# Attention of a decoder block: probabilities and values exchanged through DRAM, with the scores of two steps as four products in a row

## The reference

```python
scale = DIM_HEAD ** (-0.5)                      # DIM_HEAD = 64, HEADS = 16
xn = layer_norm(x, ln_g, ln_b)                  # [32, 112, 256]
cn = layer_norm(context, cln_g, cln_b)          # [32, 375, 256]
q = (xn @ Wq).reshape(b, n, HEADS, DIM_HEAD).transpose(0, 2, 1, 3) * scale
k, v = jnp.split(cn @ Wkv, 2, axis=-1)          # one head of keys and values for all 16
sim = jnp.einsum('bhid,bjd->bhij', q, k) + mask[:, None, :, :]
attn = jax.nn.softmax(sim, axis=-1)
out = jnp.einsum('bhij,bjd->bhid', attn, v)
out = out.transpose(0, 2, 1, 3).reshape(b, n, INNER) @ Wout
h = xn @ W1
val, gate = jnp.split(h, 2, axis=-1)
out = out + jax.nn.silu(gate) * val @ W2
```

## Time and profile before

| | |
|---|---|
| median of 3 runs | 2093.75 us (2090.76 to 2095.71) |
| the profiled execution's own time | 2093.83 us |
| its span from first to last instruction | 2092.0 us |
| TensorE busy | 1724.8 us, 82% |
| VectorE busy | 1346.2 us, 64% |
| ScalarE busy | 974.7 us, 47% |
| mean share of the 16 DMA engines on the kernel's queue | 37.1% |

### The profile page before, as it was taken

How to read it: one execution, slowest core, us unless ns; L and a number is a source line. 1 busy time by engine, 2 the same in 40 slices (tenths; PEclk the granted TensorE clock), 3 DMA queues, 4 the chain that set the end, 5 groups by cost and what they waited for, 6 DMA issues and landing times. The chain is left out here.

```text
span 2092.0 us, 25897 instructions
## 1 busy us (share of the span) xinstructions
PE 1724.8 (82%) x7880; PEld 908.4 (43%) x7880; DVE 1346.2 (64%) x3972; ACT 974.7 (47%) x2262; POOL 419.4 (20%) x569
## 2 busy tenths in 40 slices
PE   5579999999996668878878877887888787888786
PEld 2447676676663223333333333333433333333355
DVE  6888999899656555655466465556646656564643
ACT  3355445544335455445455544545544554453541
POOL 4867686768500100000000000000000000000000
PEclk8789999999997879989899989999999999899998
DMA  3000000000144654545454554544554455454531
GB/s 126 1 18 10 27 10 27 19 28 2 35 147 117 185 125 118 130 103 127 121 130 108 142 117 116 133 118 120 124 127 112 117 125 128 107 124 116 118 82 37
DMA packets 153005, 197.33 MB, mean 94 GB/s; under 512 B 56513, under 2 KB 113793, under 8 KB 151969
## 3 DMA queue, kind: packets, MB, share of 16 engines
q1 hardware_dynamic: 152400, 195.21, 37.1%
q10 hardware_dynamic: 464, 0.46, 0.1%
HBM read 96.92 MB, written 7.42 MB: 50 GB/s over the span
## 5 line engine op out<-in xcount | busy, mean ns | idle before, releaser
L1749 ACT ACTIVATE x_pr<-x_pr,x_mx 128x375 f32<-128x375 f32 x448 | 268.3, 599 | 493.4 <-DVE x_mx L1875 493.4
L1875 DVE CUSTOM_DVE_ANT_0 x_pr<-ps,x_mk 128x375 f32<-128x375 f32 x448 | 227.4, 545 | 266.0 <-issue 141.8
L1554 PE MATMUL ps<-x_xn,x_w 128*128 128x448 f32 x512 | 255.1, 634 | 89.8 <-DVE x_so L1962 37.6
L1755 ACT ACTIVATE x_pr<-x_pr,x_rc 128x375 f32<-128x375 f32 x448 | 244.2, 592 | 4.1 <-DVE x_rc L1881 4.1
L1530 PE MATMUL ps<-x_pT,x_va 128*64 128x512 f32 (+1 forms) x768 | 176.6, 600 | 65.5 <-DMA x_pT<-x_blk 65.5
L1892 DVE STREAM_TRANSPOSE x_blk<-x_pr 128x384 f32<-128x384 f32 x448 | 227.8, 547 | 0.0
L1513 PE MATMUL ps<-x_kT,x_qT 64*128 64x375 f32 x896 | 208.7, 545 | 2.6 <-issue 2.4
L1554 PEld LDWEIGHTS ps<-x_xn,x_w 128*128 128x128 f32 x512 | 103.4, 216 | 211.3 <-issue 99.9
L314 PE MATMUL ps<-m_xa,w_in 128*128 128x448 f32 x352 | 146.5, 564 | 6.2 <-ACT m_xa L532 6.2
L1905 DVE TENSOR_TENSOR x_cT<-x_cT,x_rb 128x375 f32<-128x375 f32 x64 | 32.0, 541 | 163.9 <-DMA x_rb<-context_roots 163.9
L1554 PE MATMUL ps<-f_xn,f_w 128*128 128x448 f32 x224 | 100.4, 577 | 39.3 <-DVE x_ff L1947 21.0
(11 more groups left out here) (194 smaller groups left out, 2817.3 us busy)
## 6 DMA issues: line engine op xcount, KB each, us to landing
x_pT<-x_blk SPq DMA_DIRECT2D x512, 96.0 KB, 2.1
x_mk<-in_mask SPq DMA_DIRECT2D x224, 187.5 KB, 4.5
x_pT<-x_blk SPq DMA_DIRECT2D x512, 72.0 KB, 2.1
x_cx<-in_context SPq DMA_DIRECT2D x32, 375.0 KB
x_cT<-in_context_turned SPq DMA_DIRECT2D x32, 375.0 KB, 5.1
x_rb<-context_roots SPq DMA_DIRECT2D x32, 187.5 KB, 5.3
x_va<-x_vT SPq DMA_DIRECT2D x256, 12.0 KB, 1.8
m_Rd<-bc_roots SPq DMA_DIRECT2D x8, 448.0 KB, 3.5
```

Source lines behind the costliest of these rows:

```text
L1554: last = pe.matmul(to[:, 0:T], weights[:, k, at:at + 128], moving[:, k, :], start=(k == 0), stop=(k == KD - 1))
L1749: act.activation(pr[:, k, 0:J], pr[:, k, 0:J], ACT.Exp, scale=-1.0, bias=mx[:, k:k + 1], accum_out=sums[:, k:k + 1]).then_inc(h_e.sem, 1)
L1755: act.activation(pr[:, k + e, 0:J], pr[:, k + e, 0:J], ACT.Copy, scale=rc[:, k + e:k + e + 1]).then_inc(h_n.sem, 1)
L1875: dve.tensor_tensor_reduce(pr[:, k + e, 0:J], bank(2 * (p % 2) + e)[:, 0:J], mk[:, p % SLOT, :], -1.0, 3.0e38, ALU.add, ALU.min, mx[:, k + ...
```

## The change

The exchange of blocks goes through DRAM. After every step, one transfer stores that step's turned blocks (`blocks_out`, from all 128 partitions); after the last step of a set, 4 transfers load them into place (`blocks_in`, each into 32 partitions). `pT` exists twice, and the staging tile `blocks` three times, a step each. The values take two stores and two loads (`values_out`, `values_in`, the latter now at step 0 of the batch itself). `turn` runs one step earlier: VectorE does `divide(p)` at the end of step p and `turn(p - 1)` right after `highest(p)`, and ScalarE does `scaled(p - 1)` ahead of `exps(p)`. TensorE issues the scores of steps p and p + 1 together in even steps.

```diff
-            if p % NP not in (NV - 1, NP - 1):
-                return
-            n = batch(p)
-            part = JC * BLK * width_of(n)
-            sp.wait_ge(h_t.sem, h_t.value(i, 2 * p + 2))
-            hold(sp, h_o, i, n)
-            for r in range(RB):
-                for q in range(RB):
-                    sp.dma_start(pT[BLK * q:BLK * q + BLK, r * part:(r + 1) * part],
-                                 blocks[n % 2][BLK * r:BLK * r + BLK, q * part:(q + 1) * part]).then_inc(l_pt.sem, 16)
+        def blocks_out(i, p):
+            m = i * STEPS + p
+            sp.wait_ge(h_t.sem, h_t.value(i, 2 * p + 2))
+            if p % NP in (0, NV):
+                hold(sp, h_o, i, batch(p) - 1)
+            sp.dma_start(turned_dram[batch(p) % NB][:, :, p % NP % NV, :].rearrange("q p x -> p q x"),
+                         blocks[:, m % STAGES, :].rearrange("p (q x) -> p q x", q=RB)).then_inc(l_ps[m % STAGES].sem, 16)
+        def blocks_in(i, p):
+            if p % NP not in (NV - 1, NP - 1):
+                return
+            n = batch(p)
+            for k in range(p - STAGES + 1, p + 1):
+                told(sp, l_ps, i, k)
+            hold(sp, h_o, i, n - 1)
+            for q in range(RB):
+                sp.dma_start(pT[n % NB][BLK * q:BLK * q + BLK].rearrange("p r s t w b -> p r (s t w b)"),
+                             turned_dram[n % NB][q].rearrange("(r a) s x -> a r (s x)", a=BLK)).then_inc(l_pt.sem, 16)
...
+        def values_out(i, b):
+            sp.wait_ge(c_t.sem, c_t.value(i, b + 1))
+            for k in range(DH // BLK):
+                sp.dma_start(values_dram[:, :, k, :].rearrange("q y x -> y q x"),
+                             vT[BLK * k:BLK * k + BLK, :].rearrange("p (q x) -> p q x", q=RB)).then_inc(l_vs.sem, 16)
         def values_in(i, b):
-            sp.wait_ge(c_t.sem, c_t.value(i, b + 1))
+            sp.wait_ge(l_vs.sem, l_vs.value(i, 16 * VPARTS * (b + 1)))
             hold(sp, h_o, i, NB * (b - 1))
             for k in range(DH // BLK):
-                for q in range(RB):
-                    sp.dma_start(va[BLK * q:BLK * q + BLK, b % 2, :, BLK * k:BLK * k + BLK],
-                                 vT[BLK * k:BLK * k + BLK, q * JC * BLK:(q + 1) * JC * BLK].rearrange("p (t d) -> p t d", d=BLK)).then_inc(l_va[b % 2].sem, 16)
+                sp.dma_start(va[:, b % 2, :, BLK * k:BLK * k + BLK],
+                             values_dram[:, :, k, :].rearrange("q y (t x) -> (q y) t x", x=BLK)).then_inc(l_va[b % 2].sem, 16)
...
         (SyncE, step p)
-                if p >= 3 or not first:
-                    turned_across(*back(it, p, 3))
+                if p >= 2 or not first:
+                    blocks_out(*back(it, p, 2))
+                if p >= 3 or not first:
+                    blocks_in(*back(it, p, 3))
...
+                if r == 0 and not (first and b == 0):
+                    values_in(it, b)
...
         def scores(i, p):
-            b, r = divmod(p, NP)
-            for n in range(2) if p == 0 else (p + 1,) if p < NP else ():
-                emptied(pe, i - 1 if n < QUERIES or i == 0 else i, ("query", n))
-            if r == 0:
-                emptied(pe, made_in(i, b), ("kv", b))
-            hold(pe, h_m, i, 2 * p - 2)
+            for n in range(3) if p == 0 else (p + 1, p + 2) if p < NP - 1 else ():
+                if n < KA:
+                    emptied(pe, i - 1 if n < QUERIES or i == 0 else i, ("query", n))
+            for b in range(GB):
+                if p <= NP * b < p + 2:
+                    emptied(pe, made_in(i, b), ("kv", b))
+            hold(pe, h_m, i, 2 * p)
+            for p in (p, p + 1):
+                two_scores(i, p)
...
         (TensorE, step p)
-                scores(it, p)
+                if p % 2 == 0:
+                    scores(it, p)
...
         (ScalarE, step p)
-                exps(it, p)
                 if p >= 1 or not first:
                     scaled(*back(it, p, 1))
+                exps(it, p)
...
         def turn(i, p):
-            if r in (0, NV):
-                hold(dve, l_pt, i, 16 * PARTS * (n - 1))
+            m = i * STEPS + p
+            told(dve, l_ps, 0, m - STAGES)
...
         (VectorE, step p)
                 highest(it, p)
                 if p >= 1 or not first:
-                    divide(*back(it, p, 1))
-                if p >= 2 or not first:
-                    turn(*back(it, p, 2))
+                    turn(*back(it, p, 1))
...
+                divide(it, p)
```

More of the change, by code:

```diff
@@ L1060 @@
 LAG = 5
-PARTS = RB * RB
+SW = 2 * JW
 CONTEXT = (0, 1, 4)
-VPARTS = DH // BLK * RB
+VPARTS = DH // BLK
+STAGES = 3
 CROOT = 2 * JT + 1 + RSQRT
@@ L1220, in attention @@
     rc = sb("x_rc", [ROWS, 2 * SLOT])
-    blocks = [sb(f"x_blk{n}", [ROWS, JW * 2 * width]) for n, width in enumerate((NV, NP - NV))]
-    pT = sb("x_pT", [128, JW * 2 * NV])
+    blocks = sb("x_blk", [ROWS, STAGES, SW])
+    pT = [sb(f"x_pT{n}", [128, RB, width, JC, 2, BLK]) for n, width in enumerate((NV, NP - NV))]
     OT = [sb("x_OT0", [128, GB, KA * S])]
@@ L1255, in attention @@
     c_t = count("c_t", GB)
-    l_pt = count("x_lpt", 16 * PARTS * NB * GB)
+    l_ps = [count(f"x_lps{n}", 0) for n in range(STAGES)]
+    l_pt = count("x_lpt", 16 * RB * NB * GB)
+    l_vs = count("x_lvs", 16 * VPARTS * GB)
     l_rs = count("x_lrs", 16 * GB)
@@ L1328, in batch, with told @@
         return p // NP * NB + p % NP // NV
-    def width_of(n):
-        return 2 * (NV if n % 2 == 0 else NP - NV)
+    def told(eng, sems, i, p):
+        m = i * STEPS + p
+        if m >= 0:
+            eng.wait_ge(sems[m % STAGES].sem, 16 * (m // STAGES + 1))
     def half(ap, h):
@@ L1485, in sync @@
         tokens_out(LAST - 2)
+        values_out(0, 0)
         values_in(0, 0)
@@ L1490, in sync @@
         group(NG - 1, last=True)
-        turned_across(NG - 1, STEPS - 1)
+        for p in (STEPS - 2, STEPS - 1):
+            blocks_out(NG - 1, p)
+            blocks_in(NG - 1, p - 1)
+        blocks_in(NG - 1, STEPS - 1)
         for h in range(2):
@@ L1519, in times_v @@
             m = batch(p)
-            pe.wait_ge(l_pt.sem, l_pt.value(i, 16 * PARTS * (m + 1)))
+            pe.wait_ge(l_pt.sem, l_pt.value(i, 16 * RB * (m + 1)))
             if r == NV - 1:
@@ L1526, in times_v @@
             n = r % NV + 1
-            turned = pT[:, 0:JW * width_of(m)].rearrange("p (r t w b) -> p r t w b", r=RB, t=JC, b=BLK)
             for t in range(JC):
                 for e in range(2):
-                    last = pe.matmul(bank(4)[DH * e:DH * e + DH, 0:n * ROWS], va[:, b % 2, t, :], turned[:, :, t, e::2, :].rearrange("p r n b -> p n r b"),
+                    last = pe.matmul(bank(4)[DH * e:DH * e + DH, 0:n * ROWS], va[:, b % 2, t, :], pT[m % NB][:, :, :, t, e, :].rearrange("p r s b -> p s r b"),
                                      start=(t == 0), stop=(t == JC - 1))
@@ L2057, in vector @@
         group(NG - 1, last=True)
-        turn(NG - 1, STEPS - 2)
+        turn(NG - 1, STEPS - 1)
         end_back(0)
-        divide(NG - 1, STEPS - 1)
         end_norm(0, 0)
-        turn(NG - 1, STEPS - 1)
         end_norm(0, 1)
@@ L2078, in program @@
     roots = nc.dram_tensor("context_roots", (JP, JT), FP32, kind="Internal").ap()
+    turned_blocks = [nc.dram_tensor(f"turned_blocks{n}", (RB, ROWS, width, JC * 2 * BLK), FP32, kind="Internal").ap() for n, width in enumerate((NV, NP - NV))]
+    turned_values = nc.dram_tensor("turned_values", (RB, BLK, DH // BLK, JC * BLK), FP32, kind="Internal").ap()
     with ExitStack() as ctx:
@@ L2085, in program @@
         mix = mixer(nc, ctx, PS, ident, i_in, x, xm, bc_roots, w)
-        att = attention(nc, ctx, PS, apart, ident, xm, ctx_dram, ctx_turned, roots, mask_dram, out, w)
+        att = attention(nc, ctx, PS, apart, ident, xm, ctx_dram, ctx_turned, roots, turned_blocks, turned_values, mask_dram, out, w)
         block = ctx.enter_context(nc.Block())
```

13 lines of the change are left out of this document (6 added, 7 removed).

## The result

The kernel after takes 1951.51 us in the median of four runs (1948.70 to 1955.52), the one before 2093.28 beside it: a ratio of 0.932, 95% interval 0.930 to 0.935. The forecast was 1925 us with a range of 1865 to 2000. The gain is 142 us where 168 were summed up.

A forecast was written before the change was run, and what follows sets the result against it. The bound was TensorE's work plus about 35 us standstill a group, 14.4 from SyncE's list length. Terms of -22 us a full group (six: -132), last -14, first -22 gave -168 from 2093.8: 1926, forecast 1925 us, range 1865 to 2000.

The forecast's parts named there:

- the roots' wait: TensorE's waits on `x_cT` and `x_so` in a full group go nearly to zero: -14.4 us, -8 at worst.
- early scaling: ScalarE scales ahead of the exponentials, so the tanh comes 1.09 us earlier: `x_ff` waits -5 us a group (0 to -10).
- what gets tighter: TensorE's early scores wait for maxima (no cost), query tiles and `kv`: +4.5 us a full group (0 to +10).
- four scores in a row: TensorE's scores of two steps together save half of 0.15 us a pair at most: -2 us a full group.
- The clock: TensorE's stretches at half clock behind three waits a full group go: -5 us, 0 at worst.
- slower rival: The chain through DRAM takes longer than 12.2 us; beyond 4 us the clock falls too: 2182 us at 4; chance 0.07.
- The product with the values: Block exchange through DRAM takes 12.3 us at the upper bound, the same as now, so 4.6 us for `x_pT` stay.
- The DMA share: New block stores bring the DMA engines from 0.50 to about 0.85 of a full group, just hidden behind TensorE.
- The rival of late blocks: Queued DMA engines make `x_pT` late in most of 56 sets: 67 us given back, 1990 us; chance 0.15.
- The first group: In the first group, 18 us of TensorE's waits and 4 of clock go, `x_pT` waits stay: -22 us.
- The roots still late: `x_rb` queues behind 1.1 to 1.5 MB, its wait shrinks by a third only: 2025 us; chance 0.07.
- More comes free: The `x_ff` and `x_pT` waits vanish whole: a further -8 us a group, 1870 us; chance 0.15.

## Why the prediction came out as it did

The forecast held by its main mechanism: the roots waited on the length of SyncE's list, and the matrix engine on the roots. Several of the smaller terms came near their sizes for other reasons than the ones given. Against the 22 us that I summed for a full group stand 18.3. By terms, each the six groups' difference divided by six:

| term | forecast | measured |
|---|---|---|
| the roots' wait (`x_cT` and `x_so`) | -14.4 | (24.2 - 75.8) / 6 = -8.6 |
| `x_ff` (forecast: from the early scaling) | -5 | (41.8 - 61.4) / 6 = -3.3 |
| `x_pT` | 0 | (17.1 - 27.1) / 6 = -1.7 |
| what gets tighter, and other waits | +4.5 | +4.0 |
| four scores in a row | -2 | 14 x (1.46 - 1.66) = -2.8 |
| the rest of the busy time (clock 0.92 to 0.95) | -5 | -52.3 / 6 + 2.8 = -5.9 |
| sum | -22 | -18.3 |

"What gets tighter, and other waits" is the rest of the 57.4 us of idle time. That it comes near its forecast is luck. The terms named in it did not show: the wait on `x_qT` is 4.7 us in six groups, where it was 4.9, and none for `kv` (`x_kT`) appeared in them. New or longer are `x_mx` (which I had put at nothing), `x_oT`, `x_so` L1188, `x_th` L1999 and waits that the profile calls issue.

*`x_ff`.* The early scaling is the smaller part of it. Alone it took these waits from 61.4 to 56.0 us in six groups; the rows of four alone took them to 39.4. Without the rows of four the kernel after has 54.1 (35.8 + 18.3) where it has 41.8 with them. The forecast had the rows of four only in its bound.

*The clock.* The roots' part of this term is in the kernel before with the roots on GpSimd, whose busy time fell by 20.5 us, 3.4 a group. The prediction's slower rival says that the clock falls beyond a wait of 4 us. The kernel after speaks against this as a bound: no wait of its six groups is longer than 2.6 us, and its clock was at the lower level all the same, for instance from 1027.0 to 1037.2 us, behind waits of 2.0 and 2.2 us.

*The term that was mis-sized* is the first, for two reasons. The group of the earlier trace rows had 14.4 us of these waits, but the six had 75.8, 12.6 each, so no more than that was there to gain. And "the wait goes nearly to zero" rested on `x_rb` being issued at about 1291 in before's time, 4 us after the roots were ready. I had placed the roots' write rightly (2.0 us after they were ready), and I had placed `x_rb` itself behind the block loads, but not the write: 1.5 KB issued behind 1.1 MB took 7.0 us to land, where it took at most 4.0 behind the SBUF transfers (1295.7 to 1299.8). Whether its place behind the loads in the same queue does this, or what the DMA engines had in hand, is open: from GpSimd's queue it was 5.8 us in the mean with the block loads in flight (24 batches) and 4.2 with the transfers inside SBUF. The bound that I gave for this term was -8 (half of 14.4 is 7.2); it was -8.6.

*The product with the values.* I took the upper bound, 12.3 us from store to landing, the same as before, and left the wait as it was. It fell by 1.7 us. The loads' landings ran from 3.9 to 10.1 us in the six groups, 7.1 in the median of the large ones. The estimate of 9.3 us from the Trainium skill ("SBUF — State Buffer", section on the DMA port swizzle) is of the size of the longest of these, but whatever a load stood behind in the queue is in these times too, so no run here shows the ports by themselves.

*The DMA share* was forecast at 0.85 and is 0.80. The rival of late blocks is not what happened: with 0.70 instead of 0.80 the full groups took the same time, and only with a second store per step, at 0.97, did `x_pT` rise to 40.0 us in six groups. (Six full groups have 48 sets and not the 56 that the rival counts.)

*The first group* gave 12.0 us where 22 were counted. The count was taken from 683 to 860 us, of which the last 74 us belong to the next group; in the first group itself there was no wait on `x_so`, and 15.7 us on `x_cT`. Its steps are short, and there the roots are as late as before: VectorE waits 28.2 us for `x_rb` in it after, 33.5 before, and the matrix engine's wait on `x_cT` went from 15.7 to 13.8 us. Of its gain, 8.2 us are busy time (110.75 to 102.60). The wait on `x_pT` fell from 34.5 to 21.7 us, where I had counted nothing, but new waits on `x_mx` (5.7) and `x_kT` (4.0) took most of that back. The last group gave 18.3 where 14 were counted.

*The roots still late* came true in part. The way that it names is there, queueing behind 1.1 MB, if for the write and not for `x_rb`; but VectorE's wait shrank by two thirds (112.8 to 35.2 us) and not by one. *More comes free* did not happen: the `x_ff` waits kept 41.8 of 61.4 us. *Slower through a chain in DRAM* did not come near: a store landed in 4.7 us, within a step of 5.7.

*The signs.* The roots' write came 2.0 us after the last root, as asked for (2.3 in the mean). Three more signs of being right were missed: VectorE's wait on `x_rb` is 69.6 us over the run and not under 30, the clock over the full groups 0.95 and not 0.96, a full group 160 us and not 155. And one sign of being wrong did show, VectorE's `turn` waiting for ScalarE, here over the six groups:

```profile
DVE x_blk L1922 <- ACT x_pr L1787: 43.3, 30, 2.8
```

Whether the matrix engine lost by it, no run shows.

*The scores.* No row stood behind the 0.15 us a pair that the prediction started from; measured are 0.10 a pair. Rows of four are quicker by themselves (0.20 us each) and gave 20 us alone, but nothing that can be told once the exchange and the softmax order are there: both pairs of kernels that differ in them alone are level. Part of their price is the wait on `x_pT`, which rises from 4.2 to 17.1 us in six groups.

## What to carry to other kernels

When an engine waits for a small transfer, look first at what the issuing engine had to do ahead of it, and give the small one an issuing engine that is free; here that alone was worth two thirds of a change of the whole exchange. It takes away the wait for its turn and not the time that the transfer itself takes. Count the transfers, not only the bytes: 16 issues of 0.63 us held up everything behind them while the DMA engines were half idle. Putting a small transfer further forward in the same list puts its wait ahead of the large ones too, so that needs a trial: it gave 62 us in the kernel before and lost 2% in the kernel after. And a term that comes out right is not yet understood: only kernels with one part of the change each showed which part moved the `x_ff` waits.

## What the runs showed of the hardware

A write of 1.5 KB issued right behind four loads of 288 KB in one queue had landed after 7.0 us. From its issue to the issue of the transfer that waited for it, in the mean of 24 batches: 3.8 us behind 16 small transfers inside SBUF, 7.6 behind the four loads, and from GpSimd's own queue 4.2 beside the transfers inside SBUF and 5.8 beside the loads. `x_rb`, 188 KB, took 4.8 us to land (medians over some two groups) where SyncE had issued nothing for 5 us ahead of it, 10.3 us right behind eight other issues, and on GpSimd's queue 4.2 us in the kernel before and 7.5 in the kernel after, whose DMA engines were at 0.82.

An issue by SyncE took 0.63 us for a transfer of 32 partitions to 32, and 2.07 us for four loads (0.52 each), but 2.04 us for a single one right behind eight others (1246.63 with the roots' write ahead of the loads).

Stores of 384 KB in 768-byte pieces to DRAM, the loads back and the other transfers beside them ran at 206 GB/s over the six groups with the engines at 0.80, and with the second store at 258 GB/s over one group with 0.97.

Two score products of 64 rows to 375 columns in float32, one in each half of the partitions, took 0.83 us to the start of the next product, and four in a row 1.46, at the full clock.

In the kernel before, the products behind a wait of 5.2 us (from 816.8 us on) ran at a granted clock of 0.50; in the kernel after, so did those behind two waits of 2.0 and 2.2 us that end at 1025.8 and 1028.6 us.
